# Where ScalarE takes the next batch's exponentials in the second attention

## The reference

```
q = (x @ Wq).reshape(B, Nq, HEADS, DIM_HEAD)
k = (context @ Wk).reshape(...);  v = (context @ Wv).reshape(...)
sim = jnp.einsum('bihd,bjhd->bhij', q, k) * SCALE
attn = jax.nn.softmax(sim, axis=-1)
out = jnp.einsum('bhij,bjhd->bihd', attn, v)
return out.reshape(B, Nq, HEADS * DIM_HEAD) @ Wo + bo
```

## Time and profile before

| | |
|---|---|
| runs, us | 2351.68, 2355.81, 4204.26 |
| median of the 3 | 2355.81 |
| profiled execution: time, span | 2354.85, 2353.1 |
| granted TensorE clock, mean over the span | 0.966 |
| PE, PEld, DVE, ACT, POOL busy, share of the span | 94%, 81%, 78%, 61%, 32% |
| second attention, 783 to 1083: PE, PEld, DVE, ACT busy, us of 300 | 290.97, 247.50, 263.40, 212.79 |
| exponentials of the second attention: count, us in all | 64, 45.7 |

### The profile page before, as it was taken

The page is one execution under the profiler, slowest core; times in us unless marked ns, Lnnn a source line. Parts: engine busy times, 40 slices in busy tenths (PEclk is TensorE's granted clock), DMA queues, the critical chain, the costliest instruction groups (busy, mean ns, idle before and its releaser), DMA issues.

```text
span 2353.1 us, 48867 instructions
## 1 busy us (share of the span) xinstructions
PE 2208.9 (94%) x14664; PEld 1896.6 (81%) x14669; DVE 1828.0 (78%) x4429; ACT 1441.8 (61%) x2996; POOL 755.4 (32%) x1047
## 2 busy tenths in 40 slices
PE   7899999999899999997669999999997999979999
PEld 6788888888698788885248888888886888879998
DVE  3789888898966688886977788778787676866666
ACT  6566665666344677775865666666654555636666
POOL 2355546555412122226430111111112342412333
PEclk8999999999899999998789999999998999979999
DMA  8454544545200444453234544554441000024445
GB/s 223 122 144 126 146 142 135 143 124 162 65 16 10 135 130 133 134 160 103 64 82 126 143 142 129 147 145 142 134 120 49 1 1 14 27 64 143 140 140 160
DMA packets 462543, 262.88 MB, mean 112 GB/s; under 512 B 25792, under 2 KB 442460, under 8 KB 461660
## 3 DMA queue, kind: packets, MB, share of 16 engines
q1 hardware_dynamic: 462428, 261.56, 39.6%
HBM read 153.25 MB, written 108.27 MB: 111 GB/s over the span
## 4 chain that ended last, share of the span: by engine, by line
PE 78%; DVE 10%; ACT 6%; issue 2%; DMA 1%; POOL 1%; DVEq 0%; SPq 0%; ACTq 0%; POOLq 0%
PE ps_o L1170 13%; PE ps_s L1157 11%; PE ps_t L1142 6%; PE ps_p L89 6%; PE ps_p L91 6%; PE ps_p L90 6%; PE ps_o L1877 3%; PE ps_t L1877 3%; PE ps_t L3595 2%; PE ps_s L3577 2%; PE ps_o L3595 2%; PE ps_s L89 2%; PE ps_s L91 2%; PE ps_s L90 2%; DVE a_sm L1511 2%
## 5 line engine op out<-in xcount | busy, mean ns | idle before, releaser
L1170 PEld LDWEIGHTS ps_o<-a_val,a_pt 128*128 128x128 f32 (+2 forms) x3200 | 414.7, 192 | 40.9 <-issue 10.4
L1170 PE MATMUL ps_o<-a_val,a_pt 128*128 128x128 f32 (+2 forms) x3200 | 427.3, 276 | 6.6 <-ACT a_pt L1361 3.2
L1157 PE MATMUL ps_s<-a_keys,a_zt 128*128 128x308 f32 (+1 forms) x1024 | 415.4, 492 | 5.5 <-DVE a_e L1503 3.3
L1511 DVE TENSOR_REDUCE a_sm<-a_e 128x16 f32<-128x1232 f32 (+1 forms) x192 | 234.2, 1220 | 181.9 <-ACT a_e L1369 181.5
L1331 ACT ACTIVATE a_stage<-ps_p 128x512 f32<-128x512 f32 (+1 forms) x341 | 203.8, 598 | 252.2 <-PE ps_p L91 249.8
L1361 ACT ACTIVATE a_pt<-ps_t 128x512 f32<-128x512 f32 (+1 forms) x448 | 225.1, 505 | 143.3 <-PE ps_t L1142 142.1
L1142 PE MATMUL ps_t<-ident,a_e 128*128 128x128 f32 (+1 forms) x1600 | 261.7, 276 | 27.2 <-POOL a_e L1528 13.7
L1322 ACT ACTIVATE a_keys<-ps_p 128x308 f32<-128x308 f32 x566 | 241.1, 427 | 73.2 <-PE ps_p L91 73.1
L89 PE MATMUL ps_p<-ct_hi,a_mt_hi 96*128 (+1 forms) x566 | 274.8, 486 | 0.0
L1369 ACT ACTIVATE a_e<-a_e 128x1232 f32<-128x1232 f32 (+1 forms) x192 | 204.1, 1063 | 69.5 <-DVE a_e L1503 53.4
L1528 POOL TENSOR_TENSOR a_e<-a_e,a_rs 128x539 f32<-128x539 f32 (+1 forms) x192 | 165.8, 891 | 227.4 <-DVE a_rs L1516 226.0
(11 more groups left out here) (470 smaller groups left out, 5035.0 us busy)
## 6 DMA issues: line engine op xcount, KB each, us to landing
a_vals<-a_stage SPq DMA_DIRECT2D x152, 512.0 KB, 3.5
a_val<-a_vals SPq DMA_DIRECT2D x128, 576.0 KB
f_w<-in_L_ffn_W_dram SPq DMA_DIRECT2D x129, 256.0 KB, 2.7
a_val<-a_vals SPq DMA_DIRECT2D x64, 256.0 KB
a_vals<-a_stage SPq DMA_DIRECT2D x38, 416.0 KB
a_val<-a_vals SPq DMA_DIRECT2D x128, 40.0 KB
x<-in_x_dram SPq DMA_DIRECT2D x8, 512.0 KB, 7.1
a_vals<-f_h SPq DMA_DIRECT2D x8, 512.0 KB, 4.6
```

The costliest lines, as they stand in the source:

```text
L1157: mm = eng.matmul(o, self.zt[:, par, cols], self.keys[:, par, k, h0:h0 + nh, :], start=True, stop=True)
L1170: mm = eng.matmul(c.ps_o[:, (i % 2) * P:(i % 2 + 1) * P], self.pt[0:r, n, :], self.val[0:r, i % 2, n, :], start=(n == 0), stop=(n == self. ...
L1511: eng.tensor_reduce(self.sm[:, :], e, AX.X, ALU.add).then_inc(st.sem, 1)
```

## The change

In `scalar`, the call that emits the exponentials of batch t+1 stands behind the copy of the first four turned chunks of batch t instead of ahead of it. The condition on 8 heads keeps it to the second attention.

```
-                if more and H == 8:
-                    self.exponentials(eng, t + 1, (k + 1) % 2)
                 if self.setup and not more:
                     self.after.copy_first(eng)
                 for j in range(self.uses):
                     self.copy_chunks(eng, j, self.pt, self.t_use(w, i, j, last), self.t_slot(i, j, last))
+                    if more and H == 8 and j == 0:
+                        self.exponentials(eng, t + 1, (k + 1) % 2)
                     if j < self.uses - 1:
                         copy_next(1)
```

## The result

| | before | after |
|---|---|---|
| median of 20 runs, us | 2356.19 | 2361.16 |
| ratio after / before, 95% interval | | 1.0021 (1.0015 to 1.0027) |
| profiled execution: time, span, us | 2354.85, 2353.1 | 2358.76, 2357.0 |
| a window of eight batches, us | 37.7 | 38.5 |

One of the 20 runs before, 4204.26 us, was disturbed; the ratio leaves such runs out. The ratio is 5.0 us (3.5 to 6.4) on 2356.19. I had forecast 3.5, so the sign is right and the size is at the lower edge of the interval.

A forecast was written before the change was run, and what follows sets the result against it. TensorE was taken to bound places 0 to 5, VectorE's round places 6, 7 and the last window. 3.36 + 0.2 - 0.1 = 3.5 us on 2354.85 gave 2358.3 us; range 2352 to 2364.

The forecast's parts named there:

- What bounds the kernel: Second attention: TensorE runs without gaps in places 0 to 5; VectorE's round decides in places 6, 7 and the last window.
- The price of a copy ahead of the exponentials: On ScalarE, a copy holds the exponentials up by 0.48 us, from its start to the next start.
- the two bounds: Limits on the copy's delay of the exponentials: 0 if it fits into idle time, 0.58 us if nothing overlaps.
- Place 6, the main term: Place 6 of the first seven windows: exponentials and TensorE 0.48 us later, no slack; 7 x 0.48 = 3.36 us.
- Places 3 and 4, the spill: Places 3 and 4: probabilities 0.03 us late for TensorE, counted in six windows; 0.2 us, or 0.8 by the larger bound.
- The earlier copy: TensorE's 7.8 us of waits for the copy: gain covered by VectorE's round, except 0.1 us in the last three batches.
- Late chunks: At 1024.45, where the copy waited for TensorE: exponentials held 1.43 us later, at no cost since TensorE is late itself.
- Rival 1: VectorE binds all through places 0 to 5, so place 3 counts like place 6: 6.7 us, 2361.6 us; chance 0.12.
- Rival 2: The copy is what TensorE lacks: its 7.8 us of waits go with nothing in their place, 2347.1 us; chance 0.08.
- Rival 3: Engines tied in lock step, exponentials held by TensorE's turning: 35 x 1.43 = 50 us slower, 2405 us; chance 0.04.
- Rival 4: Place 6's delay is taken up unseen, or ScalarE starts the copy in a gap: no difference, 2354.9 us; chance 0.06.

The follow-up runs named there:

- e3: Kernel before, with exponentials behind the copy in all places but 3 and 6; 2355.69 us against 2356.0, ratio 1.0000.
- e1: Kernel before, with exponentials behind the copy in place 6 of each window only; 2358.47 us against 2356.0, ratio 1.0010.
- e6: Kernel before, with exponentials in place 6 only behind the copy, the key unit and the fifth chunk; 2362.68 us against 2356.97, ratio 1.0020.
- e4: Kernel before, with row sums and squares taken ahead of the last value unit's copy; 2352.04 us against 2356.0, ratio 0.9983.
- e9: Kernel before, with e4's edit and TensorE's second key unit ahead of the scores in places 0 and 2; 2350.97 us against 2356.65, ratio 0.9977.
- e5: Changed kernel, with row sums and squares taken ahead of the last value unit's copy; 2355.65 us against 2356.97, ratio 0.9994.

## Why the prediction was right, and where its size was off

- *What bounds the kernel*: right. TensorE in places 0 to 5, VectorE's round in 6 and 7 and in the last window. e3 shows that in six places the order of the pair is free.
- *The price of a copy ahead of the exponentials, 0.48*: right; 0.47 after the change, and the two bounds were not needed.
- *Place 6, the main term, 3.36 us*: right in place, size and count. 0.48 or 0.49 per window in the change and in e1, 0.98 in e6. VectorE's idle time before its sum grew from 1.14 to 1.47 and not to 1.6, since the spill of the next point still has VectorE's shift 0.14 us late there: e1, without the spill, has 1.63.
- *Places 3 and 4, the spill, 0.2 us*: this is the term of the sum that was mis-sized. It measured 0.31 per window, 1.9 us in six. I had followed VectorE's delay to the probabilities, where TensorE's turning just escapes it (0.03, as forecast), and stopped there. The next things behind the probabilities on VectorE are the maxima and the shift, and TensorE's scores wait for that shift. The trace of before shows how close that was: TensorE's loads for the first scores of place 4 begin at 881.67 with no idle time before them, and VectorE's first shift had begun at 881.01 and lasted about 0.47, up to about 881.5. There were some 0.2 us of slack against a delay of 0.48. My bound for this term, 0.8 us, came from the copy's duration, so it missed the mechanism and not only the size.
- *The earlier copy, nothing, and 0.1 us gained at the end of the stage*: right. From the turning in place 0 of the last window to its last turning it took 31.98 us before and 31.88 after, 0.1 less; e3 gives the rest. But the reason was not the one given. I had ScalarE idle in the last window and hiding the copy; in fact place 6 of the last window grew there too, from 3.90 to 4.25 (the same in e1), and place 5 fell from 4.76 to 4.31. The 0.1 is what two larger terms leave, and that it came out is in part luck.
- *Late chunks*: no cost, not disproved. One place could not be followed: in the profile of before TensorE waits 1.40 us for values from memory at 1022.62, and in that of the change not at all. That place, place 1 of the seventh window, takes 6.33 us before and 5.40 in e3, whose windows take the same 37.7 us; so it shifts between executions. It is longest in the faster kernels (6.55 in e4, 6.95 in e9) and shortest in the slower ones (5.10 after the change, 4.70 in e6), as if part of what the windows gain or lose were taken back there. With one profile of each kernel that is not shown. It takes some 1.2 us out of the difference of the two spans, 3.9, against the 5.1 that the places add up to; the 5.0 us of the 20 runs agree with the places, but an interval of 3.5 to 6.4 holds both.
- *Rival 1, VectorE binds throughout*, gave 6.7, outside the interval. By my own count place 3 is late in six windows only, so it should have said 13 x 0.48 = 6.2, which the interval holds; the places decide against it, not the time. In place 3 the probabilities were early enough, as I had argued against it. But its core, that VectorE's lateness in place 3 costs, was right by two thirds, and the 90% occupancy was the hint. The Trainium skill's advice not to judge by matmul busy time ("Perfetto Trace Analysis", section Identifying the Most-Contended Engine) agrees with the trace here: TensorE reads 30.09 of 30.09 us busy, with the new wait of 0.25 us for VectorE at the scores of place 4 inside.
- *Rival 2* fell with the sign of the result, and with e3 for place 7. *Rival 3* did not come up in its size: ScalarE now waits 36.9 us for the turned chunks, but e3, with 29.4 us of these waits, takes the time of before, and the clock stayed at 1.00. e5 shows that such a wait can cost, by under 0.2 us a window. *Rival 4* is excluded by the interval.

Sum by what was measured: 7 x 0.48 + 6 x 0.31 - 0.1 = 5.1 us, against 5.0 (3.5 to 6.4).

## What to carry to other kernels

When one instruction of an in-order engine is put ahead of another, ask at each place of the pattern when the second could have started without the first. If the first, with its own wait for input, is through by then, the order is free, as in six places here. If not, the second is late by the difference: 0.48 us, one start-to-start time, where ScalarE came late to the pair, and 0.65 in e5 against e4, where the first had to wait for its input too. Then follow the delayed result past its first consumer, over everything behind it on the consumer's queue, since a buffer that it frees may have less slack than the data that it makes. The better edit here was to empty the queue ahead of the critical pair: 0.68 us of sums that fit into a gap of 0.94.

## What the runs showed of the hardware

Nothing new of a mechanism, but a way of measuring. From the third window to the sixth the place-to-place times of this loop agree within 0.06 us, and in the places that an edit does not touch they agree as well between kernels, in executions of 2351 to 2359 us. Effects nearly add: 0.47 and 0.29 apart, 0.79 together. An engine can read as 100% busy and still hide its waits: TensorE's 189 matmuls of places 0 to 5 read as 29.59 of 29.59 us busy before and as 29.91 of 29.91 after, with one wait of 0.25 us more.
